# Layer 2 attention of a four-layer kernel: a unit's scores in one burst, its transposes in one bank, its values in one block

## What is computed

```python
def _L2_attn_ref(x, Wq, Wk, Wv, Wo, bo):
    ...
    q = split_heads(x @ Wq)
    k = split_heads(x @ Wk)
    v = split_heads(x @ Wv)
    q = apply_rope(q)
    k = apply_rope(k)
    sim = jnp.einsum('bid,bjd->bij', q, k) * scale
    causal = jnp.tril(jnp.ones((t, t), dtype=bool))
    sim = jnp.where(causal[None], sim, -jnp.inf)
    attn = jax.nn.softmax(sim, axis=-1)
    out = jnp.einsum('bij,bjd->bid', attn, v)
    out = out.reshape(b, h, t, d).transpose(0, 2, 1, 3).reshape(b, t, h * d)
    return out @ Wo + bo
...
x = x + ga * _L2_attn_ref(h, L2_attn_Wq, L2_attn_Wk, L2_attn_Wv, L2_attn_Wo, L2_attn_bo)
```

## Time and profile before

| | |
|---|---|
| three runs, us | 1380.21, 1386.87, 1388.79 (median 1386.87) |
| profiled execution, us | span 1397.1; no time beside the span is given |
| TensorE busy | 1194.7 us, 86% |
| VectorE busy | 1006.7 us, 72% |
| ScalarE busy | 905.7 us, 65% |
| GpSimd busy | 579.6 us, 41% |
| share of TensorE in the chain that ended last | 75% |
| scores of layer 2 attention | starts from 325.0 to 685.8 us of the span |
| its transposes | starts from 337.6 to 696.7 us |

### The profile page before, as it was taken

How to read it: one execution, slowest core, us unless ns; L and a number is a source line. 1 busy time by engine, 2 the same in 40 slices (tenths; PEclk the granted TensorE clock), 3 DMA queues, 4 the chain that set the end, 5 groups by cost and what they waited for, 6 DMA issues and landing times.

```text
span 1397.1 us, 28068 instructions
## 1 busy us (share of the span) xinstructions
PE 1194.7 (86%) x10484; PEld 698.7 (50%) x10484; DVE 1006.7 (72%) x2420; ACT 905.7 (65%) x2160; POOL 579.6 (41%) x554
## 2 busy tenths in 40 slices
PE   7787048758999999999979999997889879898878
PEld 5333048743555555555524566663555543555543
DVE  3455842247989889889663899995888864788864
ACT  3564001116777777777767888884888862888862
POOL 1022035525444444444230222223787830778740
PEclk8897558969999999999999999999999999999999
DMA  9002105431000000000020000000000000000000
GB/s 330 4 0 61 57 15 185 163 100 37 1 1 1 1 0 1 1 1 2 1 106 0 2 2 2 2 2 33 2 2 2 2 2 0 2 1 2 2 2 30
DMA packets 20677, 40.68 MB, mean 29 GB/s; under 512 B 3859, under 2 KB 13595, under 8 KB 19902
## 3 DMA queue, kind: packets, MB, share of 16 engines
q1 hardware_dynamic: 18494, 37.14, 7.7%
q0 software_dynamic: 2048, 1.74, 0.5%
HBM read 33.17 MB, written 6.55 MB: 28 GB/s over the span
## 4 chain that ended last, share of the span: by engine, by line
PE 75%; DVE 9%; issue 6%; ACT 5%; POOL 2%; DMA 1%; another core or an unknown queue 1%; SPq 0%; DVEq 0%; POOLq 0%; ACTq 0%
PE bank L1115 5%; PE bank L1128 5%; PE bank L1546 5%; PE bank L1534 4%; PE pair L1084 4%; PE bank L1524 4%; PE bank L1552 4%; PE bank L2303 3%; PE bank L1102 3%; PE pair L1102 3%; PE pair L1087 2%; PE pair L1783 2%; PE bank L2018 2%; PE bank L1135 2%; PE pair L2038 2%
## 5 line engine op out<-in xcount | busy, mean ns | idle before, releaser
L1370 POOL TENSOR_TENSOR rope_part<-rope_part,rope_tab 128x512 f32<-128x512 f32 x64 | 81.6, 1274 | 188.2 <-DVE rope_part L1276 188.1
L1203 ACT ACTIVATE soft<-bank,neg_max 128x512 f32<-128x512 f32 (+2 forms) x192 | 100.4, 536 | 26.6 <-DVE neg_max L1284 26.4
L2241 POOL TENSOR_TENSOR win_part<-win_part,scaled_tab 128x512 f32<-128x512 f32 x64 | 81.8, 1278 | 77.1 <-DVE win_part L2177 76.7
L1599 POOL TENSOR_TENSOR win_soft_alibi<-win_soft_alibi,win_inv_alibi 128x384 f32<-128x384 f32 x64 | 51.7, 826 | 147.9 <-DVE win_inv_alibi L1583 147.8
L1220 ACT ACTIVATE softT<-bank 128x512 f32<-128x512 f32 x160 | 92.4, 599 | 28.7 <-PE bank L1115 28.6
L1284 DVE CUSTOM_DVE_ANT_0 bank<-bank,att_mask 128x512 f32<-128x512 f32 (+2 forms) x192 | 92.2, 522 | 5.9 <-PE bank L1102 5.9
L1102 PE MATMUL bank<-k_rope,q_rope 64*128 64x512 f32 (+3 forms) x384 | 94.4, 468 | 1.6 <-POOL k_rope L1375 1.6
L1559 ACT ACTIVATE win_soft_local<-bank,win_neg_max_local,rq 128x128 f32<-128x128 f32 x256 | 92.6, 477 | 0.0
L1115 PE MATMUL bank<-ident,soft 128*128 128x128 f32 x640 | 89.4, 278 | 0.6 <-ACT softT L1220 0.5
L279 POOL TENSOR_SCALAR h<-ln_norm,mod 128x512 f32<-128x512 f32 x28 | 24.2, 866 | 158.2 <-DVE ln_norm L263 158.2
L1314 DVE TENSOR_SCALAR soft<-soft,exp_inv 128x128 f32<-128x128 f32 (+2 forms) x160 | 87.4, 593 | 1.1
(11 more groups left out here) (406 smaller groups left out, 3391.5 us busy)
## 6 DMA issues: line engine op xcount, KB each, us to landing
moe_w<-in_moe_w SPq DMA_DIRECT2D x8, 960.0 KB
y_tok<-in_moe_w SPq DMA_DIRECT2D x8, 960.0 KB
y_dram<-zeros SPq DMA_DIRECT2D x8, 256.0 KB
htok_dram<-htok SPq DMA_DIRECT2D x2, 1024.0 KB
y_tok<-y_dram SPq DMA_DIRECT2D x8, 256.0 KB, 4.9
att_w<-in_att_w SPq DMA_DIRECT2D x1, 1536.0 KB, 8.2
att_w<-in_local_w SPq DMA_DIRECT2D x1, 1536.0 KB, 9.6
wmod<-in_wmod SPq DMA_DIRECT2D x1, 1152.0 KB, 7.8
```

The source lines that it names most:

```text
L1203: nc.scalar.activation(soft[par][:, hd, TILE_AT[t]:TILE_AT[t] + keys(t)], score_bank(u, s, hd)[:, at:at + keys(t)], ACT.Exp, scale=-1.0, b ...
L1370: nc.gpsimd.tensor_tensor(rope_part[2 * piece + 1][:, :], rope_part[2 * piece + 1][:, :], rope_tab[:, 2 * piece + 1, :], ALU.mult).then_in ...
L1599: nc.gpsimd.tensor_tensor(a["soft"][u % 2][:, js, :], a["soft"][u % 2][:, js, :], a["inv"][:, u % 2, js].unsqueeze(2).to_broadcast([128, 4 ...
L2241: nc.gpsimd.tensor_tensor(swapped, swapped, scaled_tab[:, 2 * j + 1, :], ALU.mult) \
```

## The change

Only the lists of layer 2 attention are changed; the operations on the data stay what they were, but for one product that is split.

- **Scores** of a unit are issued in one burst into five banks: tile 3 of the heads in banks 1 and 2, tiles 2 and 0 in banks 3 and 4, tile 1 of both heads in bank 5. As the two row halves of the array may not write one bank at the same time, the tile 1 products are each paired with 256 columns of the other head's tile 2, whose last 128 columns are a product of their own; `s_shared` orders the two tile 1 products. The burst waits until all eight exponentials of the unit before are done.
- **Fills** all use bank 6, so fill f needs the copy of fill f - 1. Between fills stand the v projection of unit u + 2, the q projection of unit u + 3, the output product, and the k projection of unit u + 3. q and k are thus made one unit earlier than before.
- **Values** are one block at the end of the period.
- **VectorE** does all eight maxima behind the head copy, then the rope of q, the inverse, the residual addition, three normalisations, the rope of k, the second inverse and two normalisations.
- **ScalarE** takes the exponentials in the order 3, 3 | fill 0 | v | 1 | fill 1 | 1 | fill 2 | 2, 0 | fill 3 | 2, 0 | fill 4, then its three normalisations. The exponential of tile 1 waits for both tile 1 maxima, since they share a bank, and those of tiles 2 and 0 of a head for both of theirs.

A period's order on TensorE is then: scores | fill 0, v, fill 1, q, fill 2, output, fill 3, k, fill 4 | values.

```diff
@@ -1041,9 +1041,9 @@
         next_block()
         UNITS = B * PAIRS
         TILE_AT = [64 * t * (t + 1) for t in range(TB)]
-        STEPS = [[(3, 0)], [(2, 0), (0, 384)], [(1, 0)]]
-        STEP_END = [2, 6, 8]
-        TILE_ORDER = [t for step in STEPS for t, _ in step]
+        SCORE_ORDER = [(3, 0), (3, 1), (1, 0), (1, 1), (2, 0), (0, 0), (2, 1), (0, 1)]
+        BANK_MAXED = {(3, 0): 1, (3, 1): 2, (1, 0): 4, (1, 1): 4, (2, 0): 6, (0, 0): 6, (2, 1): 8, (0, 1): 8}
+        TILES_RAW = {3: 1, 1: 2, 2: 2, 0: 2}
...
@@ -1064,11 +1064,13 @@
         def keys(t):
             return 128 * (t + 1)
 
-        def score_bank(u, s, hd):
-            return bank[1 + 2 * ((3 * u + s) % 2) + hd]
+        def score_at(t, hd):
+
+            at, col = {3: (1 + hd, 0), 1: (5, 256 * hd), 2: (3 + hd, 0), 0: (3 + hd, 384)}[t]
+            return bank[at][:, col:col + keys(t)]
 
         def stat_at(t, hd):
-            return 2 * TILE_ORDER.index(t) + hd
+            return SCORE_ORDER.index((t, hd))
 
         def added(u):
 
@@ -1088,31 +1090,39 @@
                                      start=True, stop=True)
             last.then_inc(sem("proj_raw"), 1)
 
-        def att_scores(pe, u, s):
-            if s == 0:
-                pe.wait_ge(sem("roped"), 4 * u + 4)
-                if u == 0:
-                    pe.wait_ge(sem("ln_normed"), 20)
-            if 3 * u + s >= 2:
-                before, step = divmod(3 * u + s - 2, 3)
-                pe.wait_ge(sem("s_exp"), 8 * before + STEP_END[step])
-            for t, at in STEPS[s]:
-                for hd in range(2):
-                    lo = 64 * hd
-                    last = pe.matmul(score_bank(u, s, hd)[:, at:at + keys(t)],
-                                     q_rope[u % 2][lo:lo + 64, 128 * t:128 * t + 128],
-                                     k_rope[u % 2][lo:lo + 64, 0:keys(t)], start=True, stop=True)
-            last.then_inc(sem("s_raw"), 1)
+        def att_scores(pe, u):
+
+            def product(hd, t, lo=0, hi=None):
+                hi, row = hi or keys(t), 64 * hd
+                return pe.matmul(score_at(t, hd)[:, lo:hi], q_rope[u % 2][row:row + 64, 128 * t:128 * t + 128],
+                                 k_rope[u % 2][row:row + 64, lo:hi], start=True, stop=True)
+
+            pe.wait_ge(sem("roped"), 4 * u + 4)
+            if u == 0:
+                pe.wait_ge(sem("ln_normed"), 20)
+            else:
+                pe.wait_ge(sem("s_exp"), 8 * u)
+            product(0, 2, 0, 256)
+            product(1, 1).then_inc(sem("s_shared"), 1)
+            product(0, 3)
+            product(1, 3).then_inc(sem("s_raw"), 1)
+            product(0, 2, 256, 384)
+            product(1, 2, 256, 384)
+            product(0, 0)
+            product(1, 0)
+            pe.wait_ge(sem("s_shared"), u + 1)
+            product(0, 1)
+            product(1, 2, 0, 256).then_inc(sem("s_raw"), 1)
 
         def att_transpose(pe, u, f):
             if f < 2:
                 pe.wait_ge(sem("p_normed"), u + 1)
                 pe.wait_ge(sem("p_normed_act"), 2 * u + f + 1)
-            if 5 * u + f >= 2:
-                pe.wait_ge(sem("pt_ready"), 5 * u + f - 1)
+            if 5 * u + f >= 1:
+                pe.wait_ge(sem("pt_ready"), 5 * u + f)
             for i, (hd, jc, t) in enumerate(FILLS[f]):
                 at = TILE_AT[t] + 128 * jc
-                last = pe.transpose(bank[5 + (5 * u + f) % 2][:, 128 * i:128 * i + 128],
+                last = pe.transpose(bank[6][:, 128 * i:128 * i + 128],
                                     soft[u % 2][:, hd, at:at + 128], ident[:, :])
             last.then_inc(sem("pt_raw"), 1)
 
@@ -1155,39 +1165,35 @@
 
         def att_pe(pe):
             for u in range(-2, UNITS + 1):
-                score, project, work, out = 0 <= u + 1 < UNITS, u + 2 < UNITS, 0 <= u < UNITS, u >= 1
+                score, project, work, out = 0 <= u + 1 < UNITS, u + 3 < UNITS, 0 <= u < UNITS, u >= 1
                 if score:
-                    att_scores(pe, u + 1, 0)
-                if project and u > -2:
-                    att_project(pe, u + 2, 0)
-                if score:
-                    att_scores(pe, u + 1, 1)
+                    att_scores(pe, u + 1)
                 if work:
                     att_transpose(pe, u, 0)
-                    att_transpose(pe, u, 1)
+                if u + 2 < UNITS:
+                    att_project(pe, u + 2, 2)
                 if u == UNITS - 1:
                     pe.wait_ge(sem("s_exp"), 8 * UNITS)
                     ln_variance(pe, 5, 0)
                 if u == UNITS:
                     ln_centred(pe, 5, 2)
+                if work:
+                    att_transpose(pe, u, 1)
+                if project:
+                    att_project(pe, u + 3, 0)
+                if work:
+                    att_transpose(pe, u, 2)
                 if out:
                     att_output(pe, u - 1)
                 if u == UNITS - 1:
                     ln_centred(pe, 5, 1)
                 if work:
-                    att_transpose(pe, u, 2)
-                if project and u > -2:
-                    att_project(pe, u + 2, 1)
-                if score:
-                    att_scores(pe, u + 1, 2)
+                    att_transpose(pe, u, 3)
+                if project:
+                    att_project(pe, u + 3, 1)
                 if work:
-                    att_transpose(pe, u, 3)
                     att_transpose(pe, u, 4)
-                    att_values(pe, u, (0,))
-                if project:
-                    att_project(pe, u + 2, 2)
-                if work:
-                    att_values(pe, u, (1, 3, 2))
+                    att_values(pe, u, (0, 1, 3, 2))
                 if u == UNITS - 2:
                     pe.wait_ge(sem("proj_read"), 3 * UNITS)
                     ln_centred(pe, 5, 0)
@@ -1195,15 +1201,12 @@
                     ln_variance(pe, 5, 1)
             ln_variance(pe, 5, 2)
 
-        def att_exps(act, u, s, hd):
-            par = u % 2
-            act.wait_ge(sem("s_max"), 8 * u + STEP_END[s] - (0 if hd else len(STEPS[s])))
-            for t, at in STEPS[s]:
-                n = stat_at(t, hd)
-                nc.scalar.activation(soft[par][:, hd, TILE_AT[t]:TILE_AT[t] + keys(t)],
-                                     score_bank(u, s, hd)[:, at:at + keys(t)], ACT.Exp, scale=-1.0,
-                                     bias=neg_max[:, par, n:n + 1], accum_out=exp_sum[:, par, n:n + 1]) \
-                  .then_inc(sem("s_exp"), 1)
+        def att_exp(act, u, t, hd):
+            par, n = u % 2, stat_at(t, hd)
+            act.wait_ge(sem("s_max"), 8 * u + BANK_MAXED[t, hd])
+            nc.scalar.activation(soft[par][:, hd, TILE_AT[t]:TILE_AT[t] + keys(t)], score_at(t, hd), ACT.Exp, scale=-1.0,
+                                 bias=neg_max[:, par, n:n + 1], accum_out=exp_sum[:, par, n:n + 1]) \
+              .then_inc(sem("s_exp"), 1)
 
         def norm4_act(act):
             nc.scalar.preload_act_table_set("natural_log_exp_and_others")
@@ -1217,7 +1220,7 @@
                 if f == 0 and u:
                     act.wait_ge(sem("pv_raw"), B + u)
                 act.wait_ge(sem("pt_raw"), 5 * u + f + 1)
-                nc.scalar.activation(softT[:, 512 * f:512 * f + 512], bank[5 + (5 * u + f) % 2][:, :], ACT.Copy) \
+                nc.scalar.activation(softT[:, 512 * f:512 * f + 512], bank[6][:, :], ACT.Copy) \
                   .then_inc(sem("pt_ready"), 1)
 
             def values(u):
@@ -1228,38 +1231,41 @@
                                      ACT.Copy).then_inc(sem("proj_read"), 1)
 
             def norm(u, hd, t):
-                act.wait_ge(sem("s_inv"), 2 * u + 1)
+                act.wait_ge(sem("s_inv"), 2 * u + (1 if t == 3 else 2))
                 n = stat_at(t, hd)
                 p = soft[u % 2][:, hd, TILE_AT[t]:TILE_AT[t] + keys(t)]
                 return nc.scalar.activation(p, p, ACT.Copy, scale=exp_inv[:, u % 2, n:n + 1])
 
             for u in range(-2, UNITS + 1):
-                score, project, work = 0 <= u + 1 < UNITS, u + 2 < UNITS, 0 <= u < UNITS
+                score, work = 0 <= u + 1 < UNITS, 0 <= u < UNITS
                 if score:
-                    att_exps(act, u + 1, 0, 0)
-                    att_exps(act, u + 1, 0, 1)
+                    att_exp(act, u + 1, 3, 0)
+                    att_exp(act, u + 1, 3, 1)
                 if work:
                     transposed(u, 0)
+                if u + 2 < UNITS:
+                    values(u + 2)
+                if score:
+                    att_exp(act, u + 1, 1, 0)
+                if work:
                     transposed(u, 1)
                 if score:
-                    att_exps(act, u + 1, 1, 0)
+                    att_exp(act, u + 1, 1, 1)
                 if work:
                     transposed(u, 2)
                 if score:
-                    att_exps(act, u + 1, 1, 1)
+                    att_exp(act, u + 1, 2, 0)
```

(55 more changed lines are left out.)

## The result

| | before | after |
|---|---|---|
| median of 4 runs, us | 1387.83 (1380.21 to 1396.94) | 1423.07 (1411.32 to 1427.04) |
| span of the profiled execution, us | 1397.1 | 1423.0 |

The ratio is 1.0256, 95% interval 1.0216 to 1.0297: the change makes the kernel 2.6% slower.

A forecast was written before the change was run, and what follows sets the result against it. TensorE, without a gap, was taken to bound the old kernel; VectorE held up by GpSimd the new one. 29 x 0.76 = 22.0, start +4.1, last unit but one -0.25, end +2.4: +28.3 us, forecast 1415 us, range 1380 to 1432.

The forecast's parts named there:

- The loop: Per unit of attention, a cycle VectorE, ScalarE, TensorE, VectorE, GpSimd, VectorE sets the time: 12.33 us against 11.57, +0.76.
- The near ties: VectorE normalisations issued almost level with GpSimd's rope operations: first 256- and first 128-column ones lose, last wins by 0.14 us.
- Rival B: One GpSimd hold-up fewer per unit: VectorE's 11.3 us falls under TensorE's 11.37, kernel unchanged at 1387 us; chance 0.18.
- TensorE's loop: Fills waiting for copies, then values, until the next first maximum: 11.37 us per unit, not the bound.
- the start: First scores of attention wait for both projection halves, a v copy and a rope: +4.1 us.
- the end: Last stretch of attention, where single-bank fills with nothing beside them wait 0.85 us each: +2.4 us.
- One transpose bank: Fill 1 waits for fill 0's copy behind two exponentials: TensorE idles about 0.8 us, VectorE 0.9 us.
- the last unit but one: Unit 30 to unit 31 near the end of attention, without a rope: saves 0.25 us.
- TensorE at clock 1.00: TensorE was to stay at its full clock in the changed kernel, though only some 85% busy.
- Rival A: Three array shape changes per unit in place of nine pay in full: 10.4 us per unit, 1360 us; chance 0.12.
- the term of -1.15: TensorE work saved per unit by six fewer array shape changes at 0.19 us each: -1.15 us.
- the free rates: TensorE's times within one array shape, 0.86 us per 512 columns and 0.44 per four transposes: together 9.9 us per unit.

## Why the prediction was right

**The loop.** Its steps, counted from the first maximum m, stood as forecast. In the unit shown above:

| step | forecast | after |
|---|---|---|
| copy of fill 0 starts | 2.14 | 2.11 |
| fill 1 starts | 2.79 | 2.85 |
| rope of q | 4.35 | 4.41 |
| GpSimd's multiply, addition | 5.78, 7.20 | 5.84, 7.25 |
| rope of k | 8.81 | 8.86 |
| GpSimd's second multiply | 10.24 | 10.26 |
| next first maximum | 12.33 | 12.34 |

The near ties went as the earlier trace rows had said: the first 256-column and the first 128-column normalisation lost, the last one won. Of the Trainium skill, SBUF — State Buffer, Who interferes with whom, says that whichever of the two issues first gets the shared ports for its whole instruction and the other is blocked fully. The full waits agree; that an operation whose record starts 0.03 us earlier lost doesn't. Two sizes in the loop were off and nearly cancelled: the eight maxima took 3.68 us where 3.46 was forecast, and VectorE's idle time behind them 0.73 where 0.9 was. The mean unit is 12.39 and not 12.35 mostly because the addition of `gate_bo`, once in a sequence, makes a unit of 12.57. Over the 29 units the loop cost 24.5 us where 22.0 was forecast.

**The cause.** That the hold-ups by GpSimd are what decides is shown, not only argued: taking GpSimd away gives back 0.93 us per unit in the changed kernel and nothing in the old one, and moving one rope past two normalisations gives back the same 0.93. Rival B's condition (one hold-up fewer) is that last experiment, and its price held: 11.46 where TensorE's loop had been put at 11.37. That sum took 2.36 us for the values, where its own terms (1.01 + 1.45 less 0.19) give 2.27 and 2.30 was measured with GpSimd cut short, and it started them 7.4 behind the maximum, where they start 7.55 behind it there.

The hold-ups are not the whole of the slowdown. With GpSimd cut short the attention still takes 394.0 us, 6.5 more than before: the start (+4.6) and the end (+4.8, part of it by the clock) stay, and the units between them are shorter than before.

**What was half right.** "One transpose bank" was named as what makes TensorE and then VectorE wait. It is so in the trace, but it is not the reason: with two banks the unit is the same 12.39, since the v copy is at the same place in ScalarE's queue and frees bank 0 for q. The two arrive within half a microsecond of each other, and the profile names only the one that comes last. What makes the wait is ScalarE's order, with copies behind exponentials that need this unit's maxima. Bank 0 alone does it in that run; that bank 6 alone would as well is read from the trace, where fill 1 and then q stand behind it, and not shown by a run.

**The step that was mis-sized: the end.** The forecast had -0.25 for the last unit but one and +2.4 for the end, and the trace has +2.7 and +4.7. The forecast also had TensorE at clock 1.00 throughout. It fell: 0.57 in 688 to 696 and 0.66 in 701 to 706. The forecast makes the last unit but one 11.57 - 0.25 = 11.32, and it took 14.23. The kernel with GpSimd cut short has the same lists there, since no rope is left in that unit; fill 1 starts 2.87 and fill 2 4.21 behind the maximum (2.85 and 4.19 in after); it kept the full clock and took 11.46. The one with the k rope last took 11.45, also at full clock. So the term without the clock was right to 0.15, and the lower clock cost 2.8 us here, by comparison: no run holds the clock and changes nothing else.

From unit 31 to the last output product after took 24.7; the kernel with the k rope last and the one with only fill 0's copy moved kept the full clock there and took 23.3 and 23.6, and with two banks it was 20.4. By these the single bank cost 2.9 us at the end in place of 2.4 and the lower clock 1.2 to 1.4. Of the 8.0 us between the forecast's +28.3 and the attention's +36.3, the clock's two shares are thus about 4.1 (an estimate from these rows) and the loop is 2.5. The start was right (4.1 forecast, 4.5 measured).

**The price of a shape.** Rival A and the term of -1.15 rested on 0.19 us per change, an even share of all that TensorE takes beyond the free rates. Removed, they gave 0.15 each, two and four of them alike, so some 0.4 of the 1.67 us belongs to something that stays. At that price the change could bring at best 6 x 0.15 = 0.9 us per unit (an estimate; no run reached it), and even with GpSimd and the bank both out of the way the new order gave 0.29. The Trainium skill, TensorEngine Tiling (Array Packing), Key Properties, has a drain at every change of tiling mode: these runs show a price for each change, and that it is small, but not what it consists of.

## What to carry to other kernels

Grouping an engine's work by kind lengthens the time until each of its consumers gets its part: follow one period round all engines, with every queue position, before counting the saving. When a second engine is 90% busy behind the bound, look into its busy time for waits at shared ports; they cost nothing until the order moves, and then one of them may decide. The part of such a change that pays can often be had alone: here the value block and two score steps, with the rope kept early, made the old order 1.1% faster.

## What the runs showed of the hardware

TensorE's clock fell from its upper level (2.4 GHz) to the lower (1.2 GHz) at the end of the attention. These are TensorE's rows just before and at the fall:

```profile
686.46 0.63 PE L1125 MATMUL bank<-ident,soft 128*128 128x128 f32 x4 [1.48 <-ACT softT L1223]
687.80 0.66 PE L1125 MATMUL bank<-ident,soft 128*128 128x128 f32 x4 [0.71 <-ACT softT L1223]
688.29 1.57 PE L1145 MATMUL bank<-head_out,att_wo 128*128 128x512 f32 x2
```

The output product took 1.57 us where it takes 1.02 at full clock. TensorE had been busy for 1.81 of the 4 us before, since no q projection stands between the fills any more; in the unit shown above the same stretch (547.83 to 551.83) has 2.33. An idle time of 1.67 us in every one of 28 units had left the clock at 1.00, with the engine 88% busy around it; here idle times no longer than that did not. It fell 5.0 us behind unit 30's first maximum and again 4.5 us behind unit 31's. The two kernels of the new order with GpSimd cut short and one bank fell 4.2 and 5.0 us behind unit 31's; the two with full GpSimd and another order on VectorE or ScalarE did not fall before the last output product. Less work alone doesn't explain it. These are the rows behind unit 31's first maximum (683.67) in the kernel with the k rope last:

```profile
686.54 0.63 PE L1125 MATMUL bank<-ident,soft 128*128 128x128 f32 x4 [1.46 <-ACT softT L1223]
687.86 0.66 PE L1125 MATMUL bank<-ident,soft 128*128 128x128 f32 x4 [0.69 <-ACT softT L1223]
688.35 1.02 PE L1145 MATMUL bank<-head_out,att_wo 128*128 128x512 f32 x2
```

The idle times are the same, TensorE was busy for 1.86 of the 4 us from 684.07, and the clock stayed at 1.00; it stayed there too with only fill 0's copy moved, at 1.65 of the 4 us from 707.66. What tells the falls apart stays open. The Trainium skill, TensorE: Matmul & The Clock Gate, HAM oscillation — how this bites in real kernels, sees the danger in long idle gaps of TensorE; here it took none longer than the harmless ones.

Between VectorE and GpSimd, who goes first is not settled by whose record starts first: 0.03 us ahead lost, 0.11 ahead won, and the changed kernel's ties fell the same way.
